# A graph layer's edge kernel: one quarter's source rows looked up whole, the other three gathered over all partitions

## The chip, the core and the metric

The kernel runs on one core of one Trainium2 chip, in one launch. The metric is the device time of that core in microseconds; below, all times are microseconds unless marked ns. A core has TensorE (matmuls, from SBUF into the eight PSUM banks), VectorE, ScalarE, GpSimd and SyncE (SP, which here only issues transfers), and 16 DMA engines.

## What is computed

One message layer of a graph network: 12500 nodes of 32 features, 400000 edges sorted by their destination.

```python
h = jnp.maximum(_layernorm(x, axis=-1), 0.0)
e_feat = jnp.concatenate([h[src], h[dst], edge_attr], axis=-1)   # 400000 x 96
hid = jax.nn.relu(e_feat @ W1 + b1)                               # 96 -> 64
v = hid @ W2 + b2                                                 # 64 -> 32
x_cand = jax.ops.segment_max(v, dst, num_segments=12500)
out = x + jnp.maximum(x_cand, h)
```

(In the reference the layer is called on h, so that its x is h here.)

## The kernel before

The edges are cut into four quarters (A = 4) of 100000, quarter a on partitions 32a to 32a+31 of every tile. A *pair* is two blocks of 512 edges of each quarter, 4096 edges; 96 full pairs (0 to 95), one short one (96) and four mini pairs (97 to 100) make PAIRS = 101. In a block, lane l of 32 holds 16 consecutive edges or rows.

**Where the source rows come from.** Of the 16 edges of a lane the indices of the first GATHERS = 12 go to GpSimd, which makes 24 indirect transfers a pair (12 for each block g), each of one row of 32 features for all 128 partitions, into a ring of AHEAD = 7 pairs (`src_in`). VectorE transposes them (`turn_src`) to `src_t`, feature by edge. These are the first 384 edges of a block. The last 128 edges of every block (PICKED; four quarters make WIDE = 512) are looked up on TensorE instead: `look_up` multiplies a table of all nodes' features, kept in SBUF, with one-hot matrices that ScalarE and VectorE make from the indices (`picks`). This takes 98 matmuls of 512 columns for each pair (13 table tiles, in CHUNKS of 4, 3, 3, 3) and ends in `ps_rows`; VectorE's `mask_rows` takes from it `picked_rows`, which spreads a row's features over 128 partitions. Edge rows and the first rows of nodes come by plain transfers from SP (`load_edges`, `load_first`, `load_mask`); `fill_dst` and `find_max` are scans that run along the edges with a mask.

**TensorE's order** for pair j, written out by hand: layer one of pair j, the first four tiles of the look-up for pair j+2, layer two of pair j, the other nine tiles. Layer one sums into four banks, `ps_hid[a]`, one for each quarter; block g stands on partitions 64g to 64g+63 of the bank. It adds four products: the edge rows (L954), the destination rows (L958), the gathered source rows (L964, 8 matmuls with 32 rows of weights each and 384 columns), all three with weights on the quarter's own 32 partitions, and the looked-up rows (L969, 8 matmuls of 128 rows and 128 columns). A quarter's last matmul counts up `hid_summed`; ScalarE then makes `hid` (`relu_pair`, L839) and counts `hid_made`, for which layer two waits (L1003) and before which VectorE may not put the next pair's first rows into the banks (L1298). A fp32 matmul shows as two instructions in the profile.

**Other queues.** The look-up for pair j+2 waits for pair j+1's `rows_masked` (L927). GpSimd's gathers wait for `tiles_used` so as not to run too far ahead (L684), and for `src_turned`, which frees a slot of the ring (L696). SP loads new indices for half of the ring (7 pairs, `load_indices`, L453) once the last gather of that half has landed (L607), in its fixed order in `feed`: edge rows, first rows, picks, indices, masks, then the store of the maxima. In the first 12 pairs it also copies edge rows into `run_max` (L622). In the short pair only 32 edges of the second block are gathered; mini pairs (256 edges of a quarter) are all looked up. At the end GpSimd gathers 98 columns of maxima from `run_max` (L749), the last 7 only when all pairs are stored, and VectorE adds and writes out.

Of the kernel before, what the change touches and what calls it, by code (L numbers as in the profile page):

```python
# [6 lines left out]
I16, I32, U32 = mybir.dt.int16, mybir.dt.int32, mybir.dt.uint32  # L7
# [7 lines left out]
D = 16  # L15
# [4 lines left out]
A = 4  # L20
LANES = P // A
# [14 lines left out]
GATHERED = GATHERS * LANES  # L36
PICKED = PICKS * LANES


# [15 lines left out]
def tail_start(j):  # L55
    return SHORT_AT * 2 * BLK + (j > SHORT_AT) * (SHORT + (j - SHORT_AT - 1) * MINI)
# [131 lines left out]
def build(nc, x, src, dst, edge_attr, W1, b1, W2, b2, out):  # L188
    ctx = ExitStack()
    with ctx:  # L190
# [6 lines left out]
        def sem(name):  # L197
            return ctx.enter_context(nc.semaphore(name))
# [150 lines left out]
        distance_made, act_onehot_made = sem("distance_made"), sem("act_onehot_made")  # L349
        hid_summed, hid_made, v_summed, layers_begun = sem("hid_summed"), sem("hid_made"), sem("v_summed"), sem("layers_begun")  # L350
        max_scanned, max_turned, ends_set = sem("max_scanned"), sem("max_turned"), sem("ends_set")

# [5 lines left out]
        def chunk(a):  # L358
            return slice(a * LANES, (a + 1) * LANES)
# [81 lines left out]
        def _(sp):  # L441
# [8 lines left out]
            def load_indices(j, half, loaded, last=False):  # L450
                blocks = 2 * AHEAD - 3 if last else 2 * AHEAD
                for a in range(A):
                    sp.dma_start(src_ix[chunk(a), half, :, :, :].rearrange("l s g r -> l (s g) r")[:, 0:blocks],  # L453
                                 ix_view[a][:, bass.ds(j * 2, blocks)]).then_inc(loaded, D)
                    if last:
                        sp.dma_start(src_ix[chunk(a), half, AHEAD - 2, 1, 0:1], short_ix_view[a], allow_slow_non_contiguous=True).then_inc(loaded, D)
# [35 lines left out]

            for a in range(A // 2):
                sp.dma_start(src_ix[chunk(a), 0, 0, :, :], ix_view[a][:, 0:2]).then_inc(first_ix_loaded, D)
            sp.wait_ge(first_ix_loaded, A * D)
            sp.dma_start(dst_i[1:1 + PIECE, 0:SEARCH], dst_before[0:PIECE]).then_inc(dst_loaded, D)
            sp.dma_start(dst_i[1 + PIECE:BP, 0:SEARCH], dst_before[PIECE:BP - 1]).then_inc(dst_loaded, D)
            for a in range(A):
                sp.dma_start(src_ix[chunk(a), 0, 1:AHEAD, :, :].rearrange("l s g r -> l (s g) r"), ix_view[a][:, 2:2 * AHEAD]).then_inc(early_ix_loaded, D)
# [157 lines left out]
        def _(pool):  # L657
# [34 lines left out]
            def gather_turn(turn, half, loads, last=False):  # L692
                pool.wait_ge(ix_loaded[half], loads * (A * D))
# [6 lines left out]
            pool.wait_ge(first_ix_loaded, A * D)  # L700
            gather_early(0)
            pool.wait_ge(early_ix_loaded, A * D)
            for j in range(1, RAW_PAIRS):
# [32 lines left out]
            gather_turn(TURNS - 1, 1, TURNS // 2 + 1, last=True)  # L736

# [28 lines left out]
        def _(act):  # L766
            for a in range(A // 2, A):
                act.dma_start(src_ix[chunk(a), 0, 0, :, :], ix_view[a][:, 0:2]).then_inc(first_ix_loaded, D)
            act.wait_ge(first_ix_loaded, A * D)
            act.dma_start(dst_i[0:PIECE, SEARCH:SEARCH + BE], dst_rows[0:PIECE]).then_inc(dst_loaded, D)  # L770
# [62 lines left out]

            def relu_pair(j, mini=False):
                wait(act, v_summed, j)
                rows, columns = (slice(0, HID), slice(0, MINI)) if mini else (slice(0, P), slice(0, BLK))
                for a in range(A):
                    act.wait_ge(hid_summed, j * A + (a + 1))
                    nc.scalar.activation(hid[rows, a, columns], ps_hid[a][rows, columns], ACT.Relu, bias=b1_col[rows, 0:1]).then_inc(hid_made, 1)  # L839
# [16 lines left out]

            def pair(j, slot, turn, next_again=True, after_next=True, mini=False):
                relu_pair(j, mini)
# [22 lines left out]
            for j in range(SHORT_AT, PAIRS):  # L881
                pair(j, j % 2, j // 2, next_again=j + 2 < PAIRS, after_next=j + 3 < PAIRS, mini=j > SHORT_AT)

# [17 lines left out]
        def _(pe):  # L901
# [43 lines left out]
            def layer_one(j, slot, ahead=True, short=False):  # L945
# [15 lines left out]
                gathered = [GATHERED, SHORT_GATHERED if short else GATHERED]  # L961
                for g in range(2):
# [76 lines left out]
        def _(dve):  # L1039
# [87 lines left out]

            dve.wait_ge(picks_read, (A + 3) * D)
            V.tensor_copy(pick_16[:, :], pick_i[:, :, :, :].rearrange("j g a e -> j (g a e)")).then_inc(pick_step, 1)
# [397 lines left out]
```

## Time and profile before

| | |
|---|---|
| median of 3 runs | 3179.54 (3175.47 to 3183.26) |
| the profiled execution: time | 3179.01 |
| its span (first to last instruction) | 3177.2 |
| TensorE matmuls busy | 3042.7, 96% |
| GpSimd | 2387.1, 75% |
| VectorE | 2212.8, 70% |
| ScalarE | 2182.5, 69% |
| matmuls of the look-ups (L939), busy | 2317.8 |

How to read it: a row of the timeline gives the start in us from the span's start, the length in us, the engine, the line and the operation, its output and inputs, their shapes (a matmul's weights come as rows*columns ahead of the output), and how many instructions were merged; in brackets is how long the engine had been idle before, and what ended that. PEld is the loading of weights, which runs beside matmuls. SPq and ACTq are the issues of transfers. Recorded ends of matmuls are modelled, so durations of a stage are best read from start to start. The page's first part gives each engine's busy time, its share of the span and its number of instructions.

### The profile page before, as it was taken

What the parts mean: (1) busy time and instruction counts of PE and PEld (TensorE: products, weight loads), DVE (VectorE), ACT (ScalarE), POOL (GpSimd) and SP (SyncE); (2) the same over time, 40 slices, a digit from 0 to 9 for tenths busy, and PEclk for the clock granted to TensorE, in tenths of its full rate; (3) what the DMA queues carried; (4) which work ended last, traced back from release to release, by engine and by line L of the source; (5) the groups of instructions that cost most, each with busy time, mean ns of one, the idle gap of its engine ahead of it and who ended that gap; (6) DMA issues with size and microseconds to landing.
All of it is one profiled execution on the core that took longest, in us unless ns stands there. A gap on an engine that the chain in (4) does not pass through costs nothing.

```text
span 3177.2 us, 59073 instructions
## 1 busy us (share of the span) xinstructions
PE 3042.7 (96%) x19778; PEld 2247.9 (71%) x19778; DVE 2212.8 (70%) x2474; ACT 2182.5 (69%) x2555; POOL 2387.1 (75%) x2523
## 2 busy tenths in 40 slices
PE   6999899998999999999999999999898897999996
PEld 4776677776777777777777777777676675777674
DVE  5321677776777777777777777777675775777666
ACT  3334677776777777777777777777676675777674
POOL 7777677777777777777777777777777777777776
PEclk9999999999999999999999999999999998999998
DMA  8951355444343333334443334333342443333323
GB/s 255 357 201 27 75 138 136 130 117 116 96 104 103 99 96 97 99 102 104 103 104 98 101 101 103 98 96 95 97 103 51 127 102 80 96 103 100 78 65 65
DMA packets 226637, 350.67 MB, mean 110 GB/s; under 512 B 97248, under 2 KB 147708, under 8 KB 226346
## 3 DMA queue, kind: packets, MB, share of 16 engines
q1 hardware_dynamic: 142691, 303.74, 32.6%
q0 software_dynamic: 80448, 41.33, 8.2%
q10 hardware_dynamic: 3332, 4.01, 0.5%
q14 instruction: 139, 1.14, 0.1%
q8 instruction: 27, 0.44, 0.1%
HBM read 240.36 MB, written 119.78 MB: 113 GB/s over the span
## 4 chain that ended last, share of the span: by engine, by line
PE 87%; POOL 5%; DVE 2%; issue 2%; DMA 2%; SPq 1%; ACTq 0%; ACT 0%; POOLq 0%; DVEq 0%
PE ps_rows L939 66%; PE ps_layers L913 4%; PE ps_layers L919 4%; PE ps_layers L954 3%; PE ps_layers L969 3%; PE ps_layers L1007 3%; PE ps_layers L958 3%; POOL src_in L749 3%; POOL src_in L665 2%; PE ps_layers L964 2%; SPq L463 1%; DVE onehot L1251 1%; DMA src_in<-h_dram,src_ix 1%; DMA picks<-picks_dram 0%; DMA dst_i<-in_dst_dram 0%
## 5 line engine op out<-in xcount | busy, mean ns | idle before, releaser
L665 POOL DMA_INDIRECT src_in<-h_dram,src_ix x2269 | 2144.9, 945 | 700.9 <-issue 629.5
L939 PE MATMUL ps_rows<-onehot,table 128*128 128x512 f32 x9898 | 2317.8, 393 | 54.0 <-DVE onehot L1251 54.0
L939 PEld LDWEIGHTS ps_rows<-onehot,table 128*128 128x128 f32 x9898 | 1851.1, 189 | 536.1 <-issue 109.5
L853 ACT ACTIVATE onehot<-distance 128x1024 fp32r<-128x1024 bf16 x909 | 905.4, 1049 | 686.7 <-PE ps_rows L939 681.5
L848 ACT ACTIVATE distance<-picks,below_column 128x1024 bf16<-128x1024 int16 x909 | 983.7, 1136 | 67.8 <-DMA picks<-picks_dram 67.8
L1251 DVE SCALAR_TENSOR_TENSOR onehot<-picks,column,ps_layers 128x1024 fp32r<-128x1024 int16 x404 | 507.6, 1277 | 315.7 <-PE ps_rows L939 302.3
L1301 DVE STREAM_TRANSPOSE ps_layers<-rows_in 128x512 f32<-128x512 f32 x202 | 133.2, 705 | 262.9 <-ACT hid L839 194.4
L1306 DVE TENSOR_TENSOR_SCAN dst_t<-mask_in,dst_t,ps_layers 128x512 f32<-128x512 bf16 (+1 forms) x198 | 250.6, 1266 | 7.3
L839 ACT ACTIVATE hid<-ps_layers,b_col 128x512 f32<-128x512 f32 (+1 forms) x404 | 238.1, 665 | 25.4 <-PE ps_layers L969 13.8
L1319 DVE TENSOR_TENSOR_SCAN max_t<-mask_in,max_t,ps_layers 128x512 f32<-128x512 bf16 x196 | 248.8, 1269 | 4.1 <-PE ps_layers L1007 0.2
L1269 DVE SCALAR_TENSOR_TENSOR picked_rows<-picks,fold,ps_rows 128x512 f32<-128x512 int16 x202 | 141.8, 743 | 113.8 <-PE ps_rows L939 113.8
L1324 DVE STREAM_TRANSPOSE rows_in<-max_t 128x512 f32<-128x512 f32 x202 | 216.8, 1112 | 3.5
L1292 DVE STREAM_TRANSPOSE ea_t<-rows_in 128x512 f32<-128x512 f32 x202 | 204.7, 1086 | 0.0
L825 ACT ACTIVATE signs<-ps_layers,below_node 128x640 bf16<-128x640 f32 x98 | 77.7, 793 | 170.1 <-PE ps_layers L919 162.4
L913 PE MATMUL ps_layers<-ea_t,rows_in 125*128 125x320 bf16 x980 | 153.5, 303 | 25.4 <-DVE rows_in L1076 20.5
L1286 DVE STREAM_TRANSPOSE src_t<-src_in 128x384 f32<-128x384 f32 x193 | 154.4, 871 | 25.4 <-DMA src_in<-h_dram,src_ix 25.4
L919 PE MATMUL ps_layers<-dst_t,rows_in 125*128 125x320 bf16 x980 | 151.2, 302 | 0.0
L1276 DVE COPY_PREDICATED picked_rows<-of_side,ps_rows 128x512 f32<-128x512 int16 x202 | 136.8, 732 | 18.9 <-DVE picked_rows L1269 18.6
L913 PEld LDWEIGHTS ps_layers<-ea_t,rows_in 125*128 125x128 bf16 x980 | 96.2, 99 | 66.2 <-issue 21.1
L954 PE MATMUL ps_layers<-ea_t,w_edge 32*64 32x512 f32 x1552 | 110.7, 627 | 26.4 <-DVE onehot L1251 26.4
L1260 DVE SCALAR_TENSOR_TENSOR of_side<-picks,fold,ps_layers 128x1024 int16<-128x1024 int16 x101 | 128.7, 1274 | 0.0
L1174 DVE TENSOR_SCALAR tmp<-above 128x7 f32<-128x7 f32 x14 | 2.6, 183 | 177.1 <-ACT block L827 177.1
(145 smaller groups left out, 1146.5 us busy)
## 6 DMA issues: line engine op xcount, KB each, us to landing
picks<-picks_dram SPq DMA_DIRECT2D x101, 512.0 KB
first_rows<-hid SPq DMA_DIRECT2D x100, 500.0 KB
rows_in<-in_edge_attr_dram SPq DMA_DIRECT2D x384, 128.0 KB
rows_in<-first_rows SPq DMA_DIRECT2D x384, 128.0 KB
run_max<-rows_in SPq DMA_DIRECT2D x384, 128.0 KB
src_in<-h_dram,src_ix POOLq DMA_INDIRECT x2269
mask_in<-mask_dram SPq DMA_DIRECT2D x384, 64.0 KB
run_max<-in_edge_attr_dram SPq DMA_DIRECT2D x10, 1024.0 KB
```

The lines of the kernel that those rows point to most:

```text
L665: pool.indirect_dma_start(out=src_in[:, slot, g, r, :], out_offset=None, in_=rows[:, :], in_offset=bass.IndirectOffsetOnAxis(ap=src_ix[:, ...
L839: nc.scalar.activation(hid[rows, a, columns], ps_hid[a][rows, columns], ACT.Relu, bias=b1_col[rows, 0:1]).then_inc(hid_made, 1)
L848: nc.scalar.activation(distance[:, k, :], picks[:, slot, 0, :, :].rearrange("p g w -> p (g w)"), ACT.Abs, bias=below_column[:, i:i + 1]).t ...
L853: nc.scalar.activation(onehot[:, RING_AT[c] + BY_DVE[c] + k, :, :].rearrange("p g w -> p (g w)"), distance[:, k, :], ACT.Relu, bias=1.0, s ...
L913: nc.tensor.matmul(ps_hid[j % 2 * 2 + half][:, 0:HALF + half], step[:, hb % 2, t, k * P:(k + 1) * P], rise_hi[:, t, half * HALF:(half + 1) ...
L919: mm = nc.tensor.matmul(ps_hid[j % 2 * 2 + half][:, 0:HALF], step[:, hb % 2, t, k * P:(k + 1) * P], rise_lo[:, t, half * HALF:(half + 1) * ...
L939: mm = nc.tensor.matmul(ps_rows[g][side][:, 0:WIDE], table[:, i * SIDES + side, part, :], onehot[:, RING_AT[c] + t, g, :], start=(i + part ...
L954: nc.tensor.matmul(ps_hid[a][g * HID:(g + 1) * HID, :], w_edge[chunk(a), :], ea_t[chunk(a), slot, g, :], start=True, stop=False)
L1251: compared = V.scalar_tensor_tensor(out=onehot[:, RING_AT[c] + t, :, :].rearrange("p g w -> p (g w)"), in0=picks[:, slot, 0, :, :].rearran ...
L1306: V.tensor_tensor_scan(dst_t[:, slot, g, 0:n], mask_in[:, slot, g, 0:n], ps_first[:, g, 0:n], state, ALU.min, ALU.max).then_inc(dst_filled ...
L1319: V.tensor_tensor_scan(max_t[:, g, 0:n], mask_in[:, slot, g, 0:n], v[g][:, 0:n], state, ALU.min, ALU.max).then_inc(max_scanned, 2 // len(c ...
L1324: V.transpose(max_out[:, slot, h, :, :], of_half(max_t[:, :, :], h)).then_inc(max_turned, 1)
```

## The change

For a full pair the fourth quarter (a = 3, WHOLE) has all its 512 edges of a block looked up: they fill the whole width of the look-up. The first three quarters have none looked up. Their first 384 edges of a block are gathered on their own partitions, as before; their last 128 each, 384 together, are gathered on the fourth quarter's partitions, four rows of each lane for each of the three quarters. The number of gathers (24 a pair), of look-up matmuls and the sizes of all tiles stay the same. The short pair and the mini pairs keep the old layout and order.

Layer one of a full pair now adds the looked-up rows first (2 matmuls of 512 columns, into the fourth bank, which is then done), waits for the transposed gathered rows, adds them for the three quarters on their own partitions (6 matmuls of 384 columns), waits until these six have ended (`own_summed`), and adds the rest from the fourth row group (6 matmuls of 128 columns, which read every lane's four rows out of twelve). ScalarE's activations take the fourth bank first. SP's index loads become six for each ring half instead of four, three of them in pieces of 4 indices (16 bytes) instead of 12; the first ones are three on SP and three on ScalarE's queue instead of two and two. The looked-up indices come by one transfer instead of four for the full pairs.

```diff
+WHOLE = A - 1
...
-        ix_view = [bass.AP(src.tensor, STARTS[a], [[GATHERS, LANES], [BLK, 2 * SHORT_AT + 1], [1, GATHERS]]).bitcast(U32) for a in range(A)]
+        ix_view = [bass.AP(src.tensor, STARTS[a], [[GATHERS, LANES], [BLK, 2 * SHORT_AT], [1, GATHERS]]).bitcast(U32) for a in range(WHOLE)]
+        rest_ix_view = [bass.AP(src.tensor, STARTS[a] + GATHERED, [[PICKS, LANES], [BLK, 2 * SHORT_AT], [1, PICKS]]).bitcast(U32) for a in range(WHOLE)]
+        def own_ix(a, half):
+            return src_ix[chunk(a), half, :, :, :].rearrange("l s g r -> l (s g) r")
+        def rest_ix(a, half):
+            return src_ix[chunk(WHOLE), half, :, :, a * PICKS:(a + 1) * PICKS].rearrange("l s g r -> l (s g) r")
...
-                for a in range(A):
-                    sp.dma_start(src_ix[chunk(a), half, :, :, :].rearrange("l s g r -> l (s g) r")[:, 0:blocks],
-                                 ix_view[a][:, bass.ds(j * 2, blocks)]).then_inc(loaded, D)
+                for a in range(WHOLE):
+                    sp.dma_start(own_ix(a, half)[:, 0:blocks], ix_view[a][:, bass.ds(j * 2, blocks)]).then_inc(loaded, D)
+                    sp.dma_start(rest_ix(a, half)[:, 0:blocks], rest_ix_view[a][:, bass.ds(j * 2, blocks)]).then_inc(loaded, D)
...
-            for a in range(A // 2):
-                sp.dma_start(src_ix[chunk(a), 0, 0, :, :], ix_view[a][:, 0:2]).then_inc(first_ix_loaded, D)
-            sp.wait_ge(first_ix_loaded, A * D)
+            for a in range(WHOLE):
+                sp.dma_start(own_ix(a, 0)[:, 0:2], ix_view[a][:, 0:2]).then_inc(first_ix_loaded, D)
+            sp.wait_ge(first_ix_loaded, 2 * WHOLE * D)
...
-            for a in range(A):
-                sp.dma_start(pick_i[0:SHORT_AT, :, a, :], bass.AP(src.tensor, STARTS[a] + GATHERED, [[2 * BLK, SHORT_AT], [BLK, 2], [1, PICKED]])).then_inc(picks_read, D)
+            sp.dma_start(pick_i[0:SHORT_AT, :, :, :].rearrange("j g a e -> j (g a e)"),
+                         bass.AP(src.tensor, STARTS[WHOLE], [[2 * BLK, SHORT_AT], [1, 2 * BLK]])).then_inc(picks_read, D)
...
-                for a in range(A):
-                    act.wait_ge(hid_summed, j * A + (a + 1))
+                order = list(range(A)) if mini or short else [WHOLE, *range(WHOLE)]
+                for n, a in enumerate(order):
+                    act.wait_ge(hid_summed, j * A + (n + 1))
...
+                if short:
+                    short_sources(j, slot)
+                    return
+                pe.wait_ge(rows_masked, j * MASKS + MASKS)
+                for g in range(2):
+                    mm = nc.tensor.matmul(ps_hid[WHOLE][g * HID:(g + 1) * HID, :], w_src[:, :], picked_rows[:, slot, g, :], start=False, stop=True)
+                mm.then_inc(hid_summed, 1)
                 pe.wait_ge(src_turned, j * 2 + 2)
+                for g in range(2):
+                    for a in range(WHOLE):
+                        nc.tensor.matmul(ps_hid[a][g * HID:(g + 1) * HID, 0:GATHERED], w_src[chunk(a), :], src_t[chunk(a), g, :],
+                                         start=False, stop=False).then_inc(own_summed, 1)
+                pe.wait_ge(own_summed, j * (2 * WHOLE) + 2 * WHOLE)
+                for a in range(WHOLE):
+                    for g in range(2):
+                        rest = src_t[chunk(WHOLE), g, :].rearrange("p (l r) -> p l r", r=GATHERS)[:, :, a * PICKS:(a + 1) * PICKS]
+                        mm = nc.tensor.matmul(ps_hid[a][g * HID:(g + 1) * HID, GATHERED:BLK].rearrange("p (l r) -> p l r", r=PICKS),
+                                              w_src[chunk(WHOLE), :], rest, start=False, stop=True)
+                    mm.then_inc(hid_summed, 1)
```

The other hunks adapt the counts of the waits and the loads of the short pair.

## Rows read from the trace of the kernel before

**Rows 1.** The page's first part: each engine's busy us, share of the span, instructions.
```profile
PE 3042.7 (96%) x19778; PEld 2247.9 (71%) x19778; DVE 2212.8 (70%) x2474; ACT 2182.5 (69%) x2555; POOL 2387.1 (75%) x2523
```

**Rows 2.** Timeline of TensorE, 1500 to 1560: one pair's layer one, and the next start.
```profile
1524.69 1.11 PE L954 MATMUL ps_layers<-ea_t,w_edge 32*64 32x512 f32 x16
1525.60 1.06 PE L958 MATMUL ps_layers<-dst_t,w_dst 32*64 32x512 f32 x16
1526.46 0.85 PE L964 MATMUL ps_layers<-src_t,w_src 32*64 32x384 f32 x16
1527.24 1.09 PE L969 MATMUL ps_layers<-picked_rows,w_src 128*64 128x128 f32 x16
1528.26 7.55 PE L939 MATMUL ps_rows<-onehot,table 128*128 128x512 f32 x32
...
1551.96 1.11 PE L954 MATMUL ps_layers<-ea_t,w_edge 32*64 32x512 f32 x16
```

**Rows 3.** Windows: us, busy us (instructions) of PE, PEld, DVE, ACT, POOL; clock; DMA.
```profile
1500.00:1528.00 28.00, 28.00 (x197) 20.95 (x194) 21.64 (x22) 21.23 (x24) 21.28 (x23) 1.00 0.40 100
```

**Rows 4.** Timeline of TensorE: starts of layer one of pairs 1, 12, 14 and 96.
```profile
395.54 1.11 PE L954 MATMUL ps_layers<-ea_t,w_edge 32*64 32x512 f32 x16
...
695.54 1.11 PE L954 MATMUL ps_layers<-ea_t,w_edge 32*64 32x512 f32 x16
...
761.04 1.11 PE L954 MATMUL ps_layers<-ea_t,w_edge 32*64 32x512 f32 x16
...
3061.69 1.11 PE L954 MATMUL ps_layers<-ea_t,w_edge 32*64 32x512 f32 x16
```

**Rows 5.** Timeline, 690 to 765: SP's four loads of edge rows that stood longest.
```profile
688.16 23.69 SPq L463 DMA_DIRECT2D rows_in<-in_edge_attr_dram  x4
```

**Rows 6.** Timeline of GpSimd: the gather behind its last wait, and the first of maxima.
```profile
391.04 0.94 POOL L665 DMA_INDIRECT src_in<-h_dram,src_ix  x1 [2.07 <-DVE src_t L1286]
...
3044.59 0.94 POOL L749 DMA_INDIRECT src_in<-run_max,gather_ix  x1 [0.30 <-issue]
```

**Rows 7.** Timeline, 2190 to 2290: index loads, and VectorE's longest wait there.
```profile
2250.37 1.89 SPq L453 DMA_DIRECT2D src_ix<-in_src_dram  x4
...
2256.00 1.32 DVE L1301 STREAM_TRANSPOSE ps_layers<-rows_in 128x512 f32<-128x512 f32 x2 [17.71 <-DMA mask_in<-mask_dram]
```

**Rows 8.** Timeline of the end, 3120 to 3178.
```profile
3155.91 0.26 SPq L642 DMA_DIRECT2D carry<-run_max  x1
...
3158.19 1.16 POOL L749 DMA_INDIRECT src_in<-run_max,gather_ix  x1 [0.30 <-issue]
...
3168.35 0.39 DVE L1475 TENSOR_TENSOR src_in<-src_in,ps_rows 128x224 f32<-128x224 f32 x1 [0.65 <-DMA src_in<-run_max,gather_ix]
```

**Rows 9.** Timeline of TensorE, 3088.9 to 3092: layer one of a mini pair.
```profile
3088.94 0.66 PE L981 MATMUL ps_layers<-ea_t,w_edge 32*64 32x256 f32 x8
3089.42 0.61 PE L983 MATMUL ps_layers<-dst_t,w_dst 32*64 32x256 f32 x8
3089.96 1.96 PE L987 MATMUL ps_layers<-picked_rows,w_src 128*64 128x128 f32 x16
```

**Rows 10.** Timeline, 2960 to 3178: how soon an engine goes on behind another's result.
```profile
2979.23 1.09 PE L969 MATMUL ps_layers<-picked_rows,w_src 128*64 128x128 f32 x16
...
2979.72 2.42 ACT L839 ACTIVATE hid<-ps_layers,b_col 128x512 f32<-128x512 f32 x4 [3.44 <-PE ps_layers L969]
...
3147.25 1.72 ACT L839 ACTIVATE hid<-ps_layers,b_col 64x256 f32<-64x256 f32 x4 [2.44 <-PE ps_layers L987]
...
3149.03 0.18 PEld L998 LDWEIGHTS ps_rows<-hid,w_out 64*32 64x32 f32 x8 [0.82 <-issue]
```

**Rows 11.** Timeline, 1499.5 to 1530: VectorE's masks, and ScalarE's activations of layer one.
```profile
1501.40 2.38 ACT L839 ACTIVATE hid<-ps_layers,b_col 128x512 f32<-128x512 f32 x4
...
1525.91 1.35 DVE L1276 COPY_PREDICATED picked_rows<-of_side,ps_rows 128x512 f32<-128x512 int16 x2 [0.16 <-DVE picked_rows L1269]
```

**Rows 12.** Timeline of the start: SP's first index loads.
```profile
0.76 0.87 SPq L494 DMA_DIRECT2D src_ix<-in_src_dram  x2
```

More of the change, by code:

```diff
@@ L37 @@
 PICKED = PICKS * LANES
+WHOLE = A - 1
+assert A * PICKED == BLK and WHOLE * PICKS == GATHERS
 MINIS = 4
@@ L350, in build @@
         hid_summed, hid_made, v_summed, layers_begun = sem("hid_summed"), sem("hid_made"), sem("v_summed"), sem("layers_begun")
+        own_summed = sem("own_summed")
         max_scanned, max_turned, ends_set = sem("max_scanned"), sem("max_turned"), sem("ends_set")
@@ L372, in build @@
         ea_view, first_view, max_view = (row_view(t) for t in (edge_attr, first_rows, run_max))
-        ix_view = [bass.AP(src.tensor, STARTS[a], [[GATHERS, LANES], [BLK, 2 * SHORT_AT + 1], [1, GATHERS]]).bitcast(U32) for a in range(A)]
+        ix_view = [bass.AP(src.tensor, STARTS[a], [[GATHERS, LANES], [BLK, 2 * SHORT_AT], [1, GATHERS]]).bitcast(U32) for a in range(WHOLE)]
+        rest_ix_view = [bass.AP(src.tensor, STARTS[a] + GATHERED, [[PICKS, LANES], [BLK, 2 * SHORT_AT], [1, PICKS]]).bitcast(U32) for a in range(WHOLE)]
+        half_ix_view = [bass.AP(src.tensor, STARTS[a] + tail_start(SHORT_AT), [[GATHERS, LANES], [1, GATHERS]]).bitcast(U32) for a in range(A)]
         short_ix_view = [bass.AP(src.tensor, STARTS[a] + tail_start(SHORT_AT) + BLK, [[1, LANES], [1, 1]]).bitcast(U32) for a in range(A)]
@@ L450, in load_indices @@
             def load_indices(j, half, loaded, last=False):
-                blocks = 2 * AHEAD - 3 if last else 2 * AHEAD
-                for a in range(A):
-                    sp.dma_start(src_ix[chunk(a), half, :, :, :].rearrange("l s g r -> l (s g) r")[:, 0:blocks],
-                                 ix_view[a][:, bass.ds(j * 2, blocks)]).then_inc(loaded, D)
-                    if last:
+                blocks = 2 * AHEAD - 4 if last else 2 * AHEAD
+                for a in range(WHOLE):
+                    sp.dma_start(own_ix(a, half)[:, 0:blocks], ix_view[a][:, bass.ds(j * 2, blocks)]).then_inc(loaded, D)
+                    sp.dma_start(rest_ix(a, half)[:, 0:blocks], rest_ix_view[a][:, bass.ds(j * 2, blocks)]).then_inc(loaded, D)
+                if last:
+                    for a in range(A):
+                        sp.dma_start(src_ix[chunk(a), half, AHEAD - 2, 0, :], half_ix_view[a]).then_inc(loaded, D)
                         sp.dma_start(src_ix[chunk(a), half, AHEAD - 2, 1, 0:1], short_ix_view[a], allow_slow_non_contiguous=True).then_inc(loaded, D)
@@ L692, in gather_turn @@
             def gather_turn(turn, half, loads, last=False):
-                pool.wait_ge(ix_loaded[half], loads * (A * D))
+                pool.wait_ge(ix_loaded[half], loads * (2 * WHOLE * D) + last * (2 * A * D))
                 pool.sem_inc(gathers_begun, 1)
@@ L698, in gather_turn @@
                     gather_pair(half, slot, turn * (AHEAD * TILES) + (slot + 2 - AHEAD) * TILES - SLACK, last and slot == AHEAD - 2)
-            pool.wait_ge(first_ix_loaded, A * D)
+            pool.wait_ge(first_ix_loaded, 2 * WHOLE * D)
             gather_early(0)
-            pool.wait_ge(early_ix_loaded, A * D)
+            pool.wait_ge(early_ix_loaded, 2 * WHOLE * D)
             for j in range(1, RAW_PAIRS):
@@ L735, in _ @@
                 gather_turn(i * 2 + 2, 0, i + 1)
-            gather_turn(TURNS - 1, 1, TURNS // 2 + 1, last=True)
+            gather_turn(TURNS - 1, 1, TURNS // 2, last=True)
             pool.wait_ge(low_row_written, D)
@@ L766, in _ @@
         def _(act):
-            for a in range(A // 2, A):
-                act.dma_start(src_ix[chunk(a), 0, 0, :, :], ix_view[a][:, 0:2]).then_inc(first_ix_loaded, D)
-            act.wait_ge(first_ix_loaded, A * D)
+            for a in range(WHOLE):
+                act.dma_start(rest_ix(a, 0)[:, 0:2], rest_ix_view[a][:, 0:2]).then_inc(first_ix_loaded, D)
+            act.wait_ge(first_ix_loaded, 2 * WHOLE * D)
             act.dma_start(dst_i[0:PIECE, SEARCH:SEARCH + BE], dst_rows[0:PIECE]).then_inc(dst_loaded, D)
@@ L832, in _, with relu_pair @@
             act.wait_ge(weights_loaded, D * (3 * A + 5))
-            def relu_pair(j, mini=False):
+            def relu_pair(j, mini=False, short=False):
                 wait(act, v_summed, j)
                 rows, columns = (slice(0, HID), slice(0, MINI)) if mini else (slice(0, P), slice(0, BLK))
-                for a in range(A):
-                    act.wait_ge(hid_summed, j * A + (a + 1))
+                order = list(range(A)) if mini or short else [WHOLE, *range(WHOLE)]
+                for n, a in enumerate(order):
+                    act.wait_ge(hid_summed, j * A + (n + 1))
                     nc.scalar.activation(hid[rows, a, columns], ps_hid[a][rows, columns], ACT.Relu, bias=b1_col[rows, 0:1]).then_inc(hid_made, 1)
@@ L854, in one_hot, with pair @@
                                          distance[:, k, :], ACT.Relu, bias=1.0, scale=-1.0).then_inc(act_onehot_made, 1)
-            def pair(j, slot, turn, next_again=True, after_next=True, mini=False):
-                relu_pair(j, mini)
+            def pair(j, slot, turn, next_again=True, after_next=True, mini=False, short=False):
+                relu_pair(j, mini, short)
                 if next_again:
@@ L881, in _ @@
             for j in range(SHORT_AT, PAIRS):
-                pair(j, j % 2, j // 2, next_again=j + 2 < PAIRS, after_next=j + 3 < PAIRS, mini=j > SHORT_AT)
+                pair(j, j % 2, j // 2, next_again=j + 2 < PAIRS, after_next=j + 3 < PAIRS, mini=j > SHORT_AT, short=j == SHORT_AT)
             act.wait_ge(onehot_made, PAIRS * DVE_ALL)
@@ L959, in layer_one, with short_sources @@
                                          start=False, stop=False)
-                pe.wait_ge(src_turned, j * 2 + 2)
-                gathered = [GATHERED, SHORT_GATHERED if short else GATHERED]
+                if short:
[5 more added lines that the diff above has]
+                mm.then_inc(hid_summed, 1)
+                pe.wait_ge(src_turned, j * 2 + 2)
+                for g in range(2):
+                    for a in range(WHOLE):
+                        nc.tensor.matmul(ps_hid[a][g * HID:(g + 1) * HID, 0:GATHERED], w_src[chunk(a), :], src_t[chunk(a), g, :],
+                                         start=False, stop=False).then_inc(own_summed, 1)
+                pe.wait_ge(own_summed, j * (2 * WHOLE) + 2 * WHOLE)
+                for a in range(WHOLE):
+                    for g in range(2):
[3 more added lines that the diff above has]
+                    mm.then_inc(hid_summed, 1)
+            def short_sources(j, slot):
+                gathered = [GATHERED, SHORT_GATHERED]
+                pe.wait_ge(src_turned, j * 2 + 2)
                 for g in range(2):
```

5 lines of the change are left out of this document (3 added, 2 removed).

## The prediction, made before the change was run

> **What bounds the kernel now.** I read the page first: TensorE is busy 96% of the span, no other engine above 75% [rows 1]. Next the timeline of TensorE in the middle of the run, for what a pair costs: layer one of one pair starts at 1524.69, of the next at 1551.96, so a pair takes 27.27 us with nothing idle, at the full granted clock, 2.4 GHz [rows 2, 3]. A busy share of 96% says that TensorE is the bound on average, not that it is at the end, so the third view is the starts of layer one over the run [rows 4]: pair 1 at 395.54, pair 96 at 3061.69. 95 pairs of 27.27 are 2590.7; the rows are 2666.2 apart. 75.5 us are idle. 11.0 of them lie between pairs 12 and 14 (65.50 us for two pairs instead of 54.54), where SP stood 23.69 us in the issue of four edge loads behind the last of the big transfers that fill run_max [rows 5]. The other 64.5 us come late, and have another cause.
>
> GpSimd makes its gathers with no wait from 391.04 (slot 8 of the ring) to 3044.59 [rows 6]. By the code these are 88 pairs of 24 and 13 of the short pair, 2125, so 1.249 us each and 29.97 us a pair: slower than TensorE by 2.70. It starts some seven pairs ahead, and after about 69 pairs the lead is gone. From then on SP, which asks for the last gather of a ring half before it loads new indices, issues those loads late (2250.37), the mask loads behind them come later still, and VectorE waits 17.71 us for a mask [rows 7]. So two engines set the end: GpSimd by its chain, TensorE with 64.5 us to spare up to pair 96. Behind pair 96 the two are tied: the last stored rows have landed at 3155.91, GpSimd asks for them at 3158.19, and VectorE's last additions wait 0.65 for the gather [rows 8].
>
> **What layer one costs, step by step.** In fp32 a matmul of N columns holds its part of the array for 4N cycles, 0.853 us for 512 columns at 2.4 GHz, and matmuls on different pieces of the array run together, also where they share rows. Three rows show it: eight 32x64 matmuls of 512 columns take 0.86 (L958 to L964); in a mini pair four of 256 columns, on half of the array, take 0.48 (L981 to L983), not a quarter of that; and eight of 128 rows whose outputs share one column half take 1.96 (L987), where the same eight over both halves take 1.09 (L969) [rows 2, 9]. From L964 to the look-ups a pair now spends 1.80: 0.64 (4 x 384) plus 0.14 before L969, 0.85 plus 0.17 before L939.
>
> **The change, part by part.**
> (a) The looked-up rows become 2 matmuls of 512 columns instead of 8 of 128: the same 0.85, since the halves g=0 and g=1 run together and the column count is equal. Fewer weight loads hide already.
> (b) The gathered rows on their own partitions: 6 matmuls instead of 8, still 384 columns each. The fourth row group stands idle; the time stays 0.64.
> (c) New: 6 matmuls of 128 columns, all of the fourth row group, two at a time: 3 x 0.213 = 0.64. Ends: 0.64 if g=0 and g=1 overlap as in L969, 1.28 if not. I take 0.64, the nearest row being that alternation.
> (d) New: TensorE waits for its own six matmuls before (c). Queued behind it are (c) and all look-ups, and behind those ScalarE and VectorE. No row has TensorE waiting for itself. The pieces: L969 began at 2979.23, its first two matmuls stream 0.27, ScalarE started at 2979.72, so 0.22 until a result is announced; TensorE's next weight load began 0.06 after ScalarE's last activation ended (3147.25 + 1.72 to 3149.03). That is 0.28 [rows 10]. Ends: 0.1 (the wait overlaps a change of shape that costs 0.14 to 0.17 anyway) to 0.63 (the second half of a batch is recorded one pass, 0.32, behind the first). I take 0.4, above the pieces, since six matmuls must report and the last start last.
> The Trainium skill has a rule that speaks against this step ("TensorE: Matmul & The Clock Gate", "The cost: per-tile semaphore tail"): increments from every tile's matmul serialize, about 26 ns each, and one on the last would do. Five more would be an estimated 0.13 on the 0.28, which makes 0.41 where the sum takes 0.4. No row here shows it.
> (e) One more change of matmul shape, 128x64 to 32x64 and later 32x64 to 128x128 where 32x64 to 128x64 to 128x128 stood: 0.14 to 0.17 by the rows, ends 0.1 and 0.25. I take 0.16.
> Sum a pair: 0.64 + 0.4 + 0.16 = 1.20 more; ends 0.84 and 1.52 with the overlap of (c).
> (f) Looked-up rows first: worth nothing. They were masked a whole pair earlier; the mask that ends at 1527.26 is that of the next pair, and gates only the look-up at 1528.26, which now moves away from it [rows 2, 11]. If that cover were gone it would cost its 1.0 us margin first.
> (g) ScalarE takes the fourth quarter first. Its four activations are bound by its own one-hots: they run without a wait [rows 11]. The last three results come up to 1.2 later than the old ones, one by one in the course of its run; at worst the run ends some 0.3 later, and the look-ups that ScalarE and VectorE then serve are 1.2 later. So nothing; without that cover, at most the 0.3.
> (h) Index loads: per ring half six issues instead of four on SP, about 0.5 each (1.89 for four [rows 7]), and 16-byte pieces for a third of the rest. The six stand ahead of the mask loads, by 1 us; in the middle of the run SP idles there. At the start one more issue on SP and on ScalarE's queue, 0.43 by the row (0.87 for two [rows 12]), before the dst loads on which the set-up hangs: 0.8, ends 0 and 2. The looked-up indices come by one transfer instead of four; far off the path.
>
> **The sum.** Pairs 0 to 95 take the new form, pair 96 and the minis don't: 96 x 1.20 = 115.2 on TensorE. A pair then takes 28.47 on TensorE, still below GpSimd's 29.97, so GpSimd never waits past its start. But TensorE now makes up only 1.50 of GpSimd's lead a pair instead of 2.70, and never catches up: layer one of pair 96 would start at about 3112, while its rows are gathered by 3045. The late idle time of 64.5 goes. Start +0.8; the stall at pair 12 shrinks by one pair's 1.2; at the end VectorE's wait of 0.65 goes, because the gather is then ready first. 115.2 - 64.5 + 0.8 - 1.2 - 0.7 = +49.6. The profiled execution has a span of 3177.2 and a time of 3179.0, and the median is 3179.5: 3229.
>
> By the same sum the break-even is 0.67 to 0.69 a pair, and each 0.1 us a pair beyond it is 9.6 us.
>
> **Rivals.**
> 1. GpSimd stays the bound: new cost a pair at or below 0.69. Then the 64.5 us of late idle time swallow all of it, and the time is the old one, 3180. For it: only 0.64 of the cost is plain streaming, and the wait could hide behind the shape change. Against: it needs the wait and the shape change together at 0.05, while each has a row of 0.14 or more. 0.11.
> 2. The two halves of (c) don't overlap, since they share a row group: 1.28 for it, 1.84 a pair, +111: 3290. For: in L958 the halves of one quarter are recorded one after the other. Against: L969 is the same alternation, and takes half of L987. The same place holds for any wait above the ends (TensorE as the bound at more than 1.5). 0.13.
> 3. It gets faster. GpSimd's chain would have to shorten, since TensorE is idle 64.5 us already and so can't be what holds the end. Its gathers stay 24 a pair of 128 rows. Only its two early waits could move, by 1 to 3 us. 0.04.
> The stall at pair 12 could vanish with slower pairs (the forecast less 10 us) if it comes from a backlog; the range holds it.
>
> **The numbers.** Forecast (TensorE bound, 0.84 to 1.52 a pair): 0.72. Its ends give 96 x 0.84 - 65.6 = +15 and 96 x 1.52 - 65.6 = +80; less and more for the stall and the start. Range 3192 to 3274; rivals 1 and 2 lie outside. A measurement tells about 0.3% (9.5 us) from no change: that much slower begins at 0.78 a pair. Faster 0.04, within 0.3% 0.12, slower 0.84.
>
> **What the profile will show.** Layer one to layer one 28.3 to 28.6 in the middle, with the gap between the own-partition matmuls and the rest near 0.4; the rest matmuls 0.64 together; the mask wait of 17.71 near 2250 gone; GpSimd's gathers still 1.249 us each, ending near 3046, and then GpSimd waiting some 50 us for the last pair to be stored. Wrong would be: a pair below 27.9 with the stalls still there (rival 1), or one near 29.1 (rival 2).

## The result, and the profile after

The changed kernel takes 3233.89 (four runs, 3230.90 to 3235.24) where the kernel before takes 3178.67 (four runs beside it): a ratio of 1.0171, with a 95% interval of 1.0158 to 1.0184. That is 55 us slower. The profiled execution of the changed kernel has a span of 3231.6 against 3177.2.

The page's first part, and the chain that ended last. L956 is now the line of the look-ups, L971 edge rows, L975 destination rows, L982 looked-up rows, L987 gathered rows on their own partitions, L993 the rest, L1046 layer two:

```profile
PE 3129.7 (97%) x19394; PEld 2224.8 (69%) x19394; DVE 2207.5 (68%) x2474; ACT 2181.9 (68%) x2555; POOL 2387.1 (74%) x2523
...
PE 95%; DVE 2%; DMA 1%; SPq 1%; issue 1%; ACTq 0%; ACT 0%; DVEq 0%
```

Against [rows 1] only TensorE has changed by much: 87 us more busy (VectorE has 5 less). GpSimd has the same 2387.1, and stands no more in the chain that ended last, of which it had 5% before.

TensorE in the middle of the run, 1500 to 1560 (start, length, operation; the bracket is idle time before it):

```profile
1518.77 1.11 PE L971 MATMUL ps_layers<-ea_t,w_edge 32*64 32x512 f32 x16
1519.68 1.06 PE L975 MATMUL ps_layers<-dst_t,w_dst 32*64 32x512 f32 x16
1520.68 1.08 PE L982 MATMUL ps_layers<-picked_rows,w_src 128*64 128x512 f32 x4
1521.69 0.89 PE L987 MATMUL ps_layers<-src_t,w_src 32*64 32x384 f32 x12
1522.81 0.87 PE L993 MATMUL ps_layers<-src_t,w_src 32*64 32x128 f32 x12 [0.24 <-PE ps_layers L987]
1523.61 7.55 PE L956 MATMUL ps_rows<-onehot,table 128*128 128x512 f32 x32
...
1547.31 1.11 PE L971 MATMUL ps_layers<-ea_t,w_edge 32*64 32x512 f32 x16
```

The answer to [rows 2]: a pair takes 28.54 between these starts (28.53 over the run) instead of 27.27, so 1.26 more. Start to start, the destination rows now take 1.00 (before 0.86, with no change of shape behind them), the looked-up rows 1.01, the own-partition rows and the wait 1.12, the rest 0.80: 3.93 from L975 to the look-ups, where the kernel before has 2.66. The rounded starts give 1.27.

Starts of layer one of pairs 1, 12, 14 and 96, as in [rows 4]:

```profile
396.30 1.11 PE L971 MATMUL ps_layers<-ea_t,w_edge 32*64 32x512 f32 x16
...
710.17 1.11 PE L971 MATMUL ps_layers<-ea_t,w_edge 32*64 32x512 f32 x16
...
776.91 1.11 PE L971 MATMUL ps_layers<-ea_t,w_edge 32*64 32x512 f32 x16
...
3116.64 1.11 PE L971 MATMUL ps_layers<-ea_t,w_edge 32*64 32x512 f32 x16
```

95 pairs of 28.533 are 2710.6, and the rows are 2720.3 apart. All that is idle is 9.7, and it lies between pairs 12 and 14 (66.74 for two pairs). The 64.5 of late idle time are gone. GpSimd, 3040 to 3212, the answer to [rows 6]:

```profile
3045.11 0.94 POOL L765 DMA_INDIRECT src_in<-run_max,gather_ix  x1 [0.30 <-issue]
...
3211.56 0.94 POOL L765 DMA_INDIRECT src_in<-run_max,gather_ix  x1 [53.14 <-SPq L657]
```

It comes to its first gather of maxima at the same time as before (3045.11 against 3044.59), because its pace is its own; and behind 91 of these gathers it waits 53.14 for the last pair to be stored. Before, it was the one that came last there.

### The profile page after: what moved, and what is told of

It reads as the page before. It is cut to its first block, busy times and chain, and to the rows that moved or that the text cites. A ratio compares the mean times of both kernels' runs of the same rounds, so it can differ in the third digit from the quotient of the medians.

```text
span 3231.6 us, 58462 instructions
## 1 busy us (share of the span) xinstructions
PE 3129.7 (97%) x19394; PEld 2224.8 (69%) x19394; DVE 2207.5 (68%) x2474; ACT 2181.9 (68%) x2555; POOL 2387.1 (74%) x2523
## 3 DMA queue, kind: packets, MB, share of 16 engines
q14 instruction: 139, 1.14, 0.1%
## 4 chain that ended last, share of the span: by engine, by line
PE 95%; DVE 2%; DMA 1%; SPq 1%; issue 1%; ACTq 0%; ACT 0%; DVEq 0%
PE ps_rows L956 70%; PE ps_layers L930 4%; PE ps_layers L936 4%; PE ps_layers L971 3%; PE ps_layers L1046 3%; PE ps_layers L982 3%; PE ps_layers L987 3%; PE ps_layers L975 3%; PE ps_layers L993 3%; SPq L478 1%; DMA picks<-picks_dram 0%; DMA dst_i<-in_dst_dram 0%; DVE onehot L1290 0%; DMA x_again<-in_x_dram 0%; ACTq L833 0%
## 5 line engine op out<-in xcount | busy, mean ns | idle before, releaser
L956 PE MATMUL ps_rows<-onehot,table 128*128 128x512 f32 x9898 | 2307.9, 392 | 10.0 <-DVE onehot L1290 10.0
L956 PEld LDWEIGHTS ps_rows<-onehot,table 128*128 128x128 f32 x9898 | 1845.1, 188 | 488.3 <-issue 109.5
L1331 DVE STREAM_TRANSPOSE ea_t<-rows_in 128x512 f32<-128x512 f32 x202 | 196.3, 1043 | 0.0
L765 POOL DMA_INDIRECT src_in<-run_max,gather_ix x98 | 92.7, 946 | 82.7 <-SPq L657 53.1
L971 PE MATMUL ps_layers<-ea_t,w_edge 32*64 32x512 f32 x1552 | 109.8, 622 | 15.3 <-DVE onehot L1290 15.3
```

What stands on the lines that cost most here:

```text
L956: mm = nc.tensor.matmul(ps_rows[g][side][:, 0:WIDE], table[:, i * SIDES + side, part, :], onehot[:, RING_AT[c] + t, g, :], start=(i + part ...
L971: nc.tensor.matmul(ps_hid[a][g * HID:(g + 1) * HID, :], w_edge[chunk(a), :], ea_t[chunk(a), slot, g, :], start=True, stop=False)
```

## The experiments

Each run has its own comparison with the kernel before, whose medians were 3178.05 to 3178.67; ratios carry a 95% interval. The price of a kernel is its pair in the middle of the run less 27.27.

### Is the whole price in the rest matmuls and their wait?

e_no_rest leaves out the rest matmuls and the wait:

```diff
-                                         start=False, stop=False).then_inc(own_summed, 1)
-                pe.wait_ge(own_summed, j * (2 * WHOLE) + 2 * WHOLE)
-                for a in range(WHOLE):
-                    for g in range(2):
...
+                                              start=False, stop=True)
+                        if g:
+                            mm.then_inc(hid_summed, 1)
```

> The changed kernel without steps (c), (d) and (e): the six matmuls of 128 columns and the wait ahead of them are left out (so the last 128 edges of three quarters lack their source rows), everything else of the change stays. Theory (the whole price lies in c, d, e): a pair is back at 27.2 to 27.4 on TensorE, the late stalls are there again, 3177 to 3183. Rival (part of the price lies in what stays: looked-up rows first, ScalarE's new order, six index loads instead of four): above 3190, with a pair above 27.5 or stalls elsewhere.

Measured: 3179.25, ratio 1.000 (0.9991 to 1.001). The time is the theory's; the pair isn't quite:

```profile
1505.96 1.11 PE L971 MATMUL ps_layers<-ea_t,w_edge 32*64 32x512 f32 x16
1506.87 1.06 PE L975 MATMUL ps_layers<-dst_t,w_dst 32*64 32x512 f32 x16
1507.86 1.08 PE L982 MATMUL ps_layers<-picked_rows,w_src 128*64 128x512 f32 x4
1508.87 0.89 PE L987 MATMUL ps_layers<-src_t,w_src 32*64 32x384 f32 x12
1509.69 7.55 PE L956 MATMUL ps_rows<-onehot,table 128*128 128x512 f32 x32
...
1533.39 1.11 PE L971 MATMUL ps_layers<-ea_t,w_edge 32*64 32x512 f32 x16
```

27.43, so 0.16 above 27.27, with (c) and (d) gone, where 27.2 to 27.4 were expected. The late stalls take it in.

### Is it the order?

e_order_only is the kernel before with the looked-up rows ahead of the gathered rows:

```diff
+                pe.wait_ge(rows_masked, j * MASKS + MASKS)
+                for a in range(A):
+                    for g in range(2):
+                        nc.tensor.matmul(ps_hid[a][g * HID:(g + 1) * HID, gathered[g]:gathered[g] + PICKED], w_src[:, :],
+                                         picked_rows[:, slot, g, a * PICKED:(a + 1) * PICKED], start=False, stop=False)
                 pe.wait_ge(src_turned, j * 2 + 2)
...
-                pe.wait_ge(rows_masked, j * MASKS + MASKS)
-                for a in range(A):
-                    for g in range(2):
...
```

> The kernel before, with the eight matmuls of looked-up rows ahead of the eight of gathered rows in the full and the short pair, nothing else. Theory (step f: the order is worth nothing, the masks are a pair early and GpSimd sets the end): a pair 27.2 to 27.4, 3176 to 3183. Rival 1 (the looked-up rows first takes a stall away, so the change had a gain that the rest hid): below 3170. Rival 2 (ScalarE gets its four banks later or closer together, and delays layer two): a pair above 27.5, but up to 0.67 of it would not show in the time; above that, over 3185.

Measured: 3178.01, ratio 0.9999 (0.999 to 1.0009). Again no change in time, and again a dearer pair (TensorE, 1502 to 1530):

```profile
1502.36 1.11 PE L954 MATMUL ps_layers<-ea_t,w_edge 32*64 32x512 f32 x16
1503.27 1.06 PE L958 MATMUL ps_layers<-dst_t,w_dst 32*64 32x512 f32 x16
1504.27 1.09 PE L964 MATMUL ps_layers<-picked_rows,w_src 128*64 128x128 f32 x16
1505.29 0.90 PE L969 MATMUL ps_layers<-src_t,w_src 32*64 32x384 f32 x16
1506.12 7.55 PE L939 MATMUL ps_rows<-onehot,table 128*128 128x512 f32 x32
...
1529.82 1.11 PE L954 MATMUL ps_layers<-ea_t,w_edge 32*64 32x512 f32 x16
```

27.46, 0.19 more, for the order alone. The destination rows and the gathered rows have one shape, and followed each other at 0.86; now 1.00 passes before the looked-up rows. A change of shape is the step to matmuls whose weights have another number of rows or columns. So the extra one, step (e), stands in the changed kernel without any rest matmuls (e_no_rest), and in the kernel before by the order alone. What counts is how many such steps the order holds: with the rest last and the own-partition rows first there are again three, as the next run shows.

### The wait, hidden and shortened

e_own_first moves the own-partition matmuls ahead of the looked-up rows, so that these lie between them and the wait:

```diff
+                pe.wait_ge(src_turned, j * 2 + 2)
+                for g in range(2):
+                    for a in range(WHOLE):
+                        nc.tensor.matmul(ps_hid[a][g * HID:(g + 1) * HID, 0:GATHERED], w_src[chunk(a), :], src_t[chunk(a), g, :],
+                                         start=False, stop=False).then_inc(own_summed, 1)
                 pe.wait_ge(rows_masked, j * MASKS + MASKS)
                 for g in range(2):
                     mm = nc.tensor.matmul(ps_hid[WHOLE][g * HID:(g + 1) * HID, :], w_src[:, :], picked_rows[:, slot, g, :], start=False, stop=True)
                 mm.then_inc(hid_summed, 1)
-                pe.wait_ge(src_turned, j * 2 + 2)
-                for g in range(2):
...
                 pe.wait_ge(own_summed, j * (2 * WHOLE) + 2 * WHOLE)
```

> The changed kernel with the six own-partition matmuls ahead of the two matmuls of looked-up rows, so that the wait for them falls behind 0.85 us of other streaming. Theory (the wait is exposed and costs 0.48 where a plain change of shape costs 0.15): the start of the rest follows 0.15 behind the end of the streaming of the looked-up rows, a pair takes 28.20 instead of 28.53, 96 x 0.33 = 32 less: 3202. Rival (the gap is that of the rest matmuls themselves, their strided reading or the swap of row groups): the gap stays 0.4 to 0.5, and the time 3234.

Measured: 3187.22, ratio 1.0031 (1.002 to 1.0043), 15 less than the theory's 3202.

```profile
1527.37 1.11 PE L971 MATMUL ps_layers<-ea_t,w_edge 32*64 32x512 f32 x16
1528.28 1.06 PE L975 MATMUL ps_layers<-dst_t,w_dst 32*64 32x512 f32 x16
1529.14 0.84 PE L983 MATMUL ps_layers<-src_t,w_src 32*64 32x384 f32 x12
1529.91 1.08 PE L987 MATMUL ps_layers<-picked_rows,w_src 128*64 128x512 f32 x4
1530.92 0.87 PE L993 MATMUL ps_layers<-src_t,w_src 32*64 32x128 f32 x12
1531.72 7.54 PE L956 MATMUL ps_rows<-onehot,table 128*128 128x512 f32 x32
...
1555.42 1.11 PE L971 MATMUL ps_layers<-ea_t,w_edge 32*64 32x512 f32 x16
```

The looked-up rows to the rest take 1.01, 0.85 and a plain change of 0.16: the wait is hidden whole, and the rival, a gap that belongs to the rest matmuls themselves, is out. The pair is 28.05, and not 28.20, because this order also gives back the change of shape between L975 and the own-partition rows (0.86 again), which the expectation had missed. What is left of the change is 0.78: 0.64 for the rest and 0.14 for a change of shape.

e_one_count keeps the change's order, but only the last of the six counts:

```diff
-                                         start=False, stop=False).then_inc(own_summed, 1)
-                pe.wait_ge(own_summed, j * (2 * WHOLE) + 2 * WHOLE)
+                                              start=False, stop=False)
+                mm.then_inc(own_summed, 1)
+                pe.wait_ge(own_summed, j + 1)
```

> The changed kernel, but of the six own-partition matmuls only the last counts own_summed up, once a pair. By the Trainium skill ('TensorE: Matmul & The Clock Gate', 'The cost: per-tile semaphore tail') five increments fewer give back an estimated 5 x 0.026 = 0.13 a pair, 12.5 in all: 3221. Rival (the increments of the first matmuls are over while the last still streams, so only the last one's counts): gap 0.48 as before, 3234.

Measured: 3222.06, ratio 1.0136 (1.012 to 1.0153).

```profile
1546.74 0.89 PE L987 MATMUL ps_layers<-src_t,w_src 32*64 32x384 f32 x12
1547.73 0.87 PE L994 MATMUL ps_layers<-src_t,w_src 32*64 32x128 f32 x12
```

0.99 instead of 1.12 from one start to the next; over the run a pair is 28.41, 0.12 less, and the time 11.8 less. Five increments gone gave 0.12 to 0.13, so 24 to 26 ns each. The rule of the Trainium skill ("TensorE: Matmul & The Clock Gate", "The cost: per-tile semaphore tail") said 26 ns each; the trace agrees, and the rival falls. The wait's 0.48 (1.12 less 0.64 of streaming) is thus 0.13 for the increments and 0.35 for the remainder.

e_own_first_one has both edits.

> The changed kernel with both edits: the six own-partition matmuls ahead of the looked-up rows, and own_summed counted once, by the last of the six. Theory (behind 0.85 of looked-up rows the wait is hidden whole, so the 0.12 that the single count gave back is gone too, and what is left of the change is 0.64 + 0.14 a pair): a pair 28.05, 3187, the same as with the first edit alone. Rival (increments hold TensorE's own stream, hidden or not): a pair 27.93 and 3179 to 3180.

Measured: 3187.61, ratio 1.003 (1.0019 to 1.0041), a pair 28.05 (1528.16 to 1556.20), as with the first edit alone. The increments cost nothing once other streaming lies over them.

### Do the two halves have to be asked for in turn?

e_rest_by_half swaps the loops of the rest:

```diff
-                for a in range(WHOLE):
-                    for g in range(2):
+                for g in range(2):
+                    for a in range(WHOLE):
```

> The changed kernel with the six matmuls of step (c) in another order: first the three for g=0, one bank after another, then the three for g=1, where the change takes g=0 and g=1 in turn. Theory (TensorE starts matmuls in order, and two run together only if both column halves of the row group are asked for one right behind the other): the first for g=1 can't start before the third for g=0, so five passes of 0.213 instead of three: 0.43 a pair more, 28.96, 3234 + 41 = 3275. Rival 1 (halves overlap in any order): 28.53 and 3234. Rival 2 (they never overlap in this order): 0.64 more a pair, 29.17, 3295.

Measured: 3261.25, ratio 1.0261 (1.0242 to 1.0279). It lies between the theory's 3275 and rival 1's 3234:

```profile
1536.00 1.14 PE L993 MATMUL ps_layers<-src_t,w_src 32*64 32x128 f32 x12 [0.24 <-PE ps_layers L987]
1537.07 7.55 PE L956 MATMUL ps_rows<-onehot,table 128*128 128x512 f32 x32
```

1.07 to the look-ups instead of 0.80: 0.27 more, where strict order would give 0.43 and free order nothing (a pair 28.81, and 96 x 0.28 = 27 is the difference in time). By the trace's records (the increments, which only the three for g=1 carry, tell them apart) the first matmul for g=1 starts 0.28 behind the first for g=0, together with the second for g=0 (0.27) and before the third (0.49), which stands ahead of it in the program. So here TensorE did start a matmul on a free column half ahead of one that waited for a busy half, but only one place ahead; whether that is a limit is left open. From 0.28 three passes of 0.213 end at 0.91, which is the 1.07 less a change of shape of 0.16; strict order would give 1.07 before that change. The Trainium skill ("TensorE: Matmul & The Clock Gate", "The mechanism") has matmuls start and end strictly in program order; this run differs from that, by the 0.28 against 0.49.

### Are there two bounds, with a break-even of 0.67 to 0.69?

e_extra_2 and e_extra_4 add look-up matmuls to the kernel before, by making the first one of each block twice or three times:

```diff
-                            for g in range(2):
+                            for n in range(2 * 2 if i + part + side == 0 else 2):
+                                g, again = n % 2, i + part + side == 0 and n < 2 * 2 - 2
...
-                                                      start=(i + part == 0), stop=(i == last_tile and part == parts - 1))
+                                                      start=(i + part == 0), stop=again or (i == last_tile and part == parts - 1))
```

(2 * 3 in e_extra_4.)

> The kernel before, with two more look-up matmuls in each pair (the first one of each block is made twice, to the same result): 2 x 0.236 = 0.47 a pair more on TensorE. Theory (two bounds, break-even at 0.67 to 0.69 a pair): it vanishes in the late stalls up to pair 96, and only some 1.4 behind pair 96 may show: 3178 to 3183. Rival (TensorE, 96% busy, is the bound throughout): 99 x 0.47 = 47 more, 3226.

> The kernel before, with four more look-up matmuls a pair: 0.94 a pair. Theory (two bounds): 96 x 0.94 = 90.5 less the 64.5 of late idle time, less 0.9 at pair 12 and 0.7 at the end, plus 2.8 behind pair 96, is +27: 3206, with no late stalls left. Rival (TensorE is the bound throughout): +93, 3272. Rival (GpSimd is the bound with more to spare than 0.67 a pair): 3180.

Measured: 3180.04 (ratio 1.0005, 0.9995 to 1.0014) and 3205.14 (1.0083, 1.0066 to 1.01). Two starts of layer one of each, e_extra_2's first:

```profile
1514.73 1.11 PE L955 MATMUL ps_layers<-ea_t,w_edge 32*64 32x512 f32 x16
...
1542.46 1.11 PE L955 MATMUL ps_layers<-ea_t,w_edge 32*64 32x512 f32 x16
```

```profile
1509.02 1.11 PE L955 MATMUL ps_layers<-ea_t,w_edge 32*64 32x512 f32 x16
...
1537.20 1.11 PE L955 MATMUL ps_layers<-ea_t,w_edge 32*64 32x512 f32 x16
```

The pairs are 27.73 and 28.18, so 0.46 and 0.91 dearer. The first disappears in the stalls, of which those at pairs 83 and 92 to 95 are left, 21.1 us of the 64.5; the second leaves none and shows what is above the break-even.

e_before_20g and e_after_20g take the other bound away: 20 gathers a pair instead of 24, in the kernel before and in the changed one.

```diff
+KEPT = GATHERS - 2
...
-                    gather_row(half, slot, n // GATHERS, n % GATHERS, rows)
+                    if n % GATHERS < kept:
+                        gather_row(half, slot, n // GATHERS, n % GATHERS, rows)
```

> The kernel before, with 20 instead of 24 gathers for every pair whose gathers are made in the ring's turns (the last two rows of each lane keep stale data, so their edges are computed from wrong rows). Theory (GpSimd's 29.97 a pair is what makes TensorE's 64.5 us of late idle time): at 24.98 a pair GpSimd waits for TensorE instead, the late stalls go, the stall at pair 12 stays: 3179 - 65 = 3114. Rival (the late stalls are SP's or VectorE's own): late stalls stay, 3170 or more.

> The changed kernel with the same four gathers a pair left out (stale data in two rows of each lane). Theory (TensorE alone is the bound after the change): the time stays, 3230 to 3236, and against the kernel before with the same gathers left out the change costs its full 96 x 1.26 = 121. Rival (GpSimd or its transfers still hold something in the changed kernel): below 3225.

Measured: 3113.65 (0.9796, 0.978 to 0.9813) and 3236.48 (1.0181, 1.0164 to 1.0198). Pairs 1 and 96 of the first, from the timeline, and two of GpSimd's waits (us in total, times, longest); then one wait of the second:

```profile
393.03 0.69 PE L956 MATMUL ps_layers<-ea_t,w_edge 32*64 32x512 f32 x8
...
2997.09 0.68 PE L956 MATMUL ps_layers<-ea_t,w_edge 32*64 32x512 f32 x8
```

```profile
POOL src_in L666 <- DVE src_t L1288: 218.9, 83, 6.6
POOL src_in L751 <- SPq L642: 95.6, 1, 95.6
```

```profile
POOL src_in L682 <- DVE src_t L1327: 324.8, 83, 6.6
```

With fewer gathers GpSimd waits for free slots of the ring, and TensorE goes from pair 1 to pair 96 in 2604.1 us: 95 x 27.27 and 13.4, of which 13.1 lie at pair 12. The late idle time of [rows 4] was made by the gathers. The edit takes away their transfers too; that the pace is GpSimd's own, and not that of the transfers, is read from its gathers at 1.249 each with no wait [rows 6]. In the changed kernel the same edit brings nothing (2.6 slower, which the spread of its runs, 3231.86 to 3237.69, covers; its median lies just above the 3236 that was expected). Between the two kernels without that bound lie 122.8 us: 96 x 1.26 is 121. This is the change's whole price; 55 of it can be seen.

All of it in one table. The last column is 3178.5 plus 96 times the price less 65.6, or 3178.5 where that is less; 65.6 is what the prediction's sum takes off.

| kernel | price a pair | time | by the two bounds |
|---|---|---|---|
| e_no_rest | 0.16 | 3179.25 | 3178.5 |
| e_order_only | 0.19 | 3178.01 | 3178.5 |
| e_extra_2 | 0.46 | 3180.04 | 3178.5 |
| e_own_first | 0.78 | 3187.22 | 3187.8 |
| e_extra_4 | 0.91 | 3205.14 | 3200.3 |
| e_one_count | 1.14 | 3222.06 | 3222.3 |
| the change | 1.26 | 3233.89 | 3233.9 |
| e_rest_by_half | 1.54 | 3261.25 | 3260.7 |

e_extra_4 lies 5 above the line. Its extra matmuls also stand in the look-ups behind pair 96 (117.4 from pair 96 to the end of the span, against 114.96 in the changed kernel) and in those ahead of pair 0.

## Why the prediction was right

Forecast 3229, measured 3233.9, inside the range and with the sign forecast. Step by step:

- (a), (b): as forecast. Looked-up rows 1.01 less a change of 0.16 is 0.85. The own-partition rows' 0.64 can't be told from the wait in the changed kernel; in e_own_first they take 0.77 with a change of shape behind them, as in [rows 2] (0.78).
- (c) 0.64, by the rest's 0.80 less its change of 0.16. Rival 2 (1.28) is out. The argument of (c), the alternation of L969, was the right one: e_rest_by_half shows that without it the step costs 0.91.
- (d) was the one term of size that was off: 0.48 against 0.4. The pieces from other rows (0.28) were too low by 0.07 even for a wait on one count (0.35), and five more increments add 0.13. Most of the 0.07 is a piece misread: 0.27 for the streaming of L969's first two matmuls, where four cycles a column, by which the 0.35 is taken, give 0.21 for 128 columns. With 0.21 the pieces make 0.34, and with the five increments 0.47. Choosing 0.4 above the pieces went the right way, but its reason gave no size: part of the nearness is luck.
- (e) 0.16 forecast, 0.15 measured in the changed kernel (0.46 for three changes against 0.31 for two). The size was right. The sequence that (e) names is that of looked-up rows first, which (f) priced at nothing, and the expectation of e_no_rest laid it to the rest matmuls; e_no_rest and e_order_only show it with no rest matmuls at all.
- (f) worth nothing, as to time: e_order_only has the time of the kernel before. But on TensorE the order isn't free: it costs 0.19 a pair, hidden there by the late idle time.
- (g) nothing, as forecast: ScalarE's four activations run without a gap (1522.75, 2.39 long, against 2.38 in [rows 11]), and e_no_rest, which keeps the new order of banks, has no dearer pair than e_order_only, which has the old one.
- (h) in the middle of the run: nothing, the six issues of a ring half delay no mask that is waited for. At the start 0.8 was forecast. Pair 1 is 0.76 later, but that holds pair 0's own price of 1.26, so the start itself is 0.5 earlier. It scatters by more than the term: less the price of pair 0, pair 1 starts at 394.1 to 396.7 in the seven kernels with the new loads, and at 392.6 to 395.5 in the three with the old ones and no matmuls added. Up to 3 us, or nothing; the runs don't settle it.
- The sum, from span to span: 96 x 1.26 = 121.0, start -0.5, late idle time -64.5, pair 12 -1.3, behind pair 96 -0.6 (114.96 against 115.51): 54.1, and the spans are 54.4 apart. The forecast was 49.6. Of the missing 4.8 the price gives 96 x 0.06 = 5.8, above all (d)'s 0.08, and the start takes 1.3 back, so that two errors partly cancel.
- The stall at pair 12 was forecast to shrink by one pair's price. It is 9.7 here, but 11.1 in e_extra_4 with slower pairs and 13.1 in e_before_20g; it scatters by more than the forecast term, and its cause, SP's issue of edge loads (23.85 here), wasn't studied.
- Rival 1 fails by its price, not by its mechanism: e_extra_2 shows just that case. Rival 3 fails with GpSimd's unchanged pace. The mask wait near 2250 is gone, and no late stall is left.

No version of the change here is as fast as the kernel before (e_before_20g is faster than both, but computes from stale rows). The nearest, e_own_first, is 0.3% slower than the kernel before: its 0.78 is 0.10 above the break-even, and what it consists of, the streaming of the rest and one change of shape, was hidden by no order tried. Even below the break-even a cheaper layer one would only reach 3178, the time that GpSimd's gathers set.

## What to carry to other kernels

Where two engines nearly tie, find each one's idle time before you price an edit: the first 65 us of TensorE work here were free, and each further one cost in full, so that "4% of this engine's work" says nothing by itself. Taking a few units of work away from the other engine shows the true price of a change in one run. Where TensorE must wait for its own results, have other work queued between; if there is none, let only the last of the results count, but only where the last one asked for is sure to end last: it was here for six equal matmuls on three row groups, and e_rest_by_half shows matmuls of one row group starting out of the program's order. Steps of one shape should stand next to each other, because each change of shape measured here, between 32x64, 128x64 and 128x128, cost TensorE 0.13 to 0.19 even where nothing waits.

## What the runs showed of the hardware

- TensorE waiting for its own six matmuls takes 0.48, of which 0.13 is five increments; with one increment 0.35; with 0.85 of other streaming between, nothing.
- In fp32, matmuls on two column halves of one row group overlap fully when they are asked for in turn (six of 128 columns in 0.64), and partly when they are asked for three and three (0.91); a later one for a free half starts ahead of an earlier one for the busy half.
- A change of shape costs 0.14 (1.00 against 0.86 for the destination rows) to 0.19 (e_order_only's gathered rows, 0.83 to the look-ups for 0.64 of streaming).
- The late stalls get fewer as TensorE's pair gets dearer: at pairs 69, 76, 83 and 91 to 95 at 27.27, at 76, 83 and 91 to 95 at 27.46 (the one at 91 only 0.4 long), at 83 and 92 to 95 at 27.73, none at 28.05.
